# Grouping the weighted sums of a fused attention and expert kernel, with a fourth probability buffer

## The chip, the cores and the metric

The kernel runs on one core of a Trainium2 chip. The metric is the device time of one launch in microseconds (us), median of three runs.

## The reference

For x of 4 batches x 1024 tokens x 256 features, both branches read the layer-normalised rows `xn`; attention has 16 heads of width 16, and each token goes to 2 of 8 experts.

```python
xn = _layernorm(x, axis=-1)
x = x + attn(xn, Wq, Wk, Wv, Wo, bo) + ffn(xn, router_logits, gating_einsum, linear, per_expert_scale, router_scale)
# attn
scores = jnp.einsum('bhqd,bhkd->bhqk', q, k)          # causal, plus the ALiBi bias, / sqrt(D)
w = jax.nn.softmax(scores, axis=-1)
ctx = jnp.einsum('bhqk,bhkd->bqhd', w, v).reshape(b, s, e)
return ctx @ Wo + bo
# ffn: softmax over 8 experts, top 2, then per expert
activation = jax.nn.gelu(gate_out[:, 0, :]) * gate_out[:, 1, :]
expert_outputs = jax.lax.ragged_dot(activation, linear.astype(dtype), group_sizes=tokens_per_expert)
```

## The kernel before, in words

The order of every engine's work is written out by hand; each engine walks its own list and waits on semaphores.

**Projection** (0 to 122.5 us) goes over 8 chunks of 512 tokens. VectorE takes means and variances (`statistics`), GpSimd makes the reciprocal roots from them (`rstds`), VectorE normalises (`normalise`, L464), TensorE transposes, and projects q, k and v. The float32 q and k are split into three bfloat16 parts: ScalarE makes the first two, GpSimd the third (L400), and SyncE stores them in device memory and loads them back as rows of `stacks`.

**Attention** (122.5 to 550 us) has 16 steps `t`, one for each batch and set of four heads. A step is cut into 18 pairs `p`. Each pair issues two score matmul groups (L753, "S" below, 512 columns each, for one head and one of the 9 units of 512 key and query columns) and between them one or two items (L745, "item" below): products for a later step from which VectorE takes row maxima (L707). Item and VectorE share two slots of PSUM: item n is only issued when VectorE is through with item n-2 (`m_taken`). ScalarE takes the exponentials of S into one of three buffers `probs` (L1090), after S has one of three PSUM banks. GpSimd masks the diagonal blocks (L883). The weighted sums (L1152, "V" below) multiply probabilities with values in float32, four heads beside each other in four column tiles of 32; a unit of 512 columns costs 16 matmul records. V of unit u stands behind pair 2u+1, with the low half of unit 2 behind pair 4, its high half and unit 3 behind pair 7: the list `PV_AT` holds nine groups of V a step. VectorE also works through some fifty operations of the routing in steps 0 to 5 (one after each odd pair), and GpSimd scatters the slot map with 8 indirect DMAs a step (L873) in steps 5 to 12. The experts' first weights `w_gu` are loaded by SyncE in steps 5 to 12.

**Experts and combination** (550 us to the end) go over 71 tiles of tokens and then add everything up.

Of the kernel before, what the change touches and what calls it, by code (L numbers as in the profile page):

```python
# [19 lines left out]
P = 128  # L20
# [17 lines left out]
CH = 512  # L38
# [50 lines left out]
PRING = 3  # L89
SRING = 3  # L90

# [11 lines left out]
PV_AT[4], PV_AT[5], PV_AT[7] = [LOW_LAST], [], [HIGH_FIRST, (3, 0), (3, 1)]  # L103
PV_LAST = [[], []] + PV_AT[:-3] + [PV_AT[-3] + PV_AT[-2] + PV_AT[-1]]
# [51 lines left out]
ROWS_AT = {(2, q): (0, (3 * q, 3 * q + 1, 3 * q + 2)) for q in range(2)} | {(4 + k, 1): (1, (2 * k, 2 * k + 1)) for k in range(3)}  # L156
# [93 lines left out]
def project(nc, ctx, ins, scratch, keep, heads, ahead):  # L250
# [64 lines left out]
    def on_sync(sp):  # L315
# [13 lines left out]
        def stores(c, par, load):  # L329
            sp.wait_ge(xn_ready, c + 1)  # L330
            sp.dma_start(xn_rows[ds(c, 1)].rearrange("a p t d -> (a p) t d"), xn[:, par]).then_inc(x_stored[par], 16)
            if load:
                sp.dma_start(x_in[:, c % XR], x_rows[c + XR]).then_inc(x_loaded[c % XR], 16)
            for q in range(NQ):
# [5 lines left out]
                if (c, q) == (2, 0):  # L340
                    for j in range(NQ):
                        sp.wait_ge(parts_stored[j], 16 + 16 * 2)
# [12 lines left out]
    def on_gpsimd(pool):  # L355
# [36 lines left out]
        for c in range(2):  # L392
            rstds(c, c)

        def body(c, par, nxt, i):
            if not nxt:
                ahead["split_maxima"](pool, 0)
            for q in range(NQ):
                pool.wait_ge(p2_ready, 4 * c + q + 1)
                pool.tensor_tensor(parts[:, q, 2], rest[:, q % 2], parts[:, q, 1], ALU.subtract).then_inc(p3_ready, 1)  # L400
            if c + 2 < NC:
                rstds(c + 2, par)

# [4 lines left out]
                           base=S - P, pattern=[[-1, S]], channel_multiplier=1).then_inc(mask_set, 1)  # L408
        early = keep["route"]
# [8 lines left out]
        for k in range(2):  # L418
            for c in range(2):
                pool.iota(keep["entries"][:, k, :, c], pattern=[[P, NT]], base=k * c * TOK, channel_multiplier=1).then_inc(mask_set, 1)  # L420
        chunks(pool, body)
# [174 lines left out]
def attend(nc, ctx, ins, scratch, keep, heads, stored):  # L596
# [3 lines left out]
    qs, ks, vals, probs = heads["qs"], heads["ks"], keep["vals"], keep["probs"]  # L600
# [210 lines left out]
    def on_sync(sp):  # L811
# [7 lines left out]
        def body(t, b, hq, has):  # L819
# [23 lines left out]
            if MAP_FROM <= t < MAP_FROM + NE:  # L843
                e = t - MAP_FROM
# [4 lines left out]
    def on_gpsimd(pool):  # L849
# [26 lines left out]
        def mask_unit(n, u):  # L876
# [4 lines left out]
            for c in DIAG[u]:  # L881
                part = probs[:, u % PRING, :, c:c + P]
# [196 lines left out]
    def on_scalar(act):  # L1079
# [4 lines left out]
        def exp(n, u, h):  # L1084
# [3 lines left out]
            if h == 0:  # L1088
                act.wait_ge(pv_done, n + 1)
# [509 lines left out]
```

## Time and profile before

| | |
|---|---|
| median of 3 runs | 816.59 us (814.65 to 817.5) |
| profiled execution | 818.57 us, span 816.8 us |
| TensorE busy | 768.0 us, 94% |
| VectorE busy | 545.4 us, 67% |
| ScalarE busy | 467.1 us, 57% |
| GpSimd busy | 429.9 us, 53% |
| mean granted TensorE clock | 0.991 |
| chain that ended last | PE 55%, issue 10%, POOL 8%, ACT 4%, DVE 4% |

Start a reading with the chain and the busy shares, and then by stage: from 122.5 to 501.7 us the fourteen attention steps 0 to 13 take 379.2 us, 26.1 to 28.7 us each. A matmul's duration in the profile is longer than its share of the array, since matmuls overlap: the distance from one start to the next is what counts.

### The profile page before, as it was taken

Reading aid. Unit: us, or ns where it says so; the run is one execution under the profiler, and the core shown is the slowest. Engines: PE = TensorE matmul, PEld = TensorE weight load, DVE = VectorE, ACT = ScalarE, POOL = GpSimd, SP = SyncE. Lnnn points to the kernel's source line nnn. Section 1 sums busy time; section 2 is a strip of 40 time slices with the busy share of each in tenths; the row PEclk is TensorE's granted clock in tenths of the full one; section 3 lists DMA queues with packets and bytes.
Section 4 is the critical chain, followed back from the end, with each engine's and each line's share of the span. In section 5 each row is a group of like instructions: output and inputs, shape, how many; then the busy total and the mean of one; then the engine's idle time right before and its main releaser. Section 6 shows DMA issues by size and latency. Waiting matters only on the chain.

```text
span 816.8 us, 17685 instructions
## 1 busy us (share of the span) xinstructions
PE 768.0 (94%) x6172; PEld 470.9 (58%) x6172; DVE 545.4 (67%) x1419; ACT 467.1 (57%) x984; POOL 429.9 (53%) x561
## 2 busy tenths in 40 slices
PE   7899999999999999999999999879899999989997
PEld 5555554444444444444444444329788888888876
DVE  5458879999999887888888888303234434334348
ACT  2565557777778677777777777874233323323310
POOL 5765542231324545645475463255586666666676
PEclk9999999999999999999999999999899999999999
DMA  8786562503233135243342350113533333322777
GB/s 199 229 253 218 170 193 74 157 17 106 82 93 85 52 95 132 51 109 100 110 98 71 94 159 16 37 40 97 139 106 108 112 116 102 111 78 87 234 237 243
DMA packets 74912, 98.20 MB, mean 120 GB/s; under 512 B 16588, under 2 KB 54092, under 8 KB 74764
## 3 DMA queue, kind: packets, MB, share of 16 engines
q1 hardware_dynamic: 65960, 78.34, 34.1%
q0 software_dynamic: 8864, 18.72, 7.4%
q8 instruction: 50, 0.82, 0.4%
q14 instruction: 38, 0.31, 0.1%
HBM read 63.53 MB, written 30.75 MB: 115 GB/s over the span
## 4 chain that ended last, share of the span: by engine, by line
PE 55%; issue 10%; POOL 8%; ACT 4%; DVE 4%; DMA 2%; another core or an unknown queue 1%; DVEq 0%; POOLq 0%; ACTq 0%
PE banks L1152 16%; PE banks L753 15%; PE banks L745 13%; PE banks L1337 7%; POOL expert_rows L1241 4%; ACT probs L1090 4%; PE banks L1346 3%; POOL stacks L592 3%; DVE stacks L1436 2%; DMA stacks<-xn_rows,places 2%; PE banks L1267 1%; DVE junk L707 1%; DMA w_gu<-expert_rows 0%; DVE probs L1319 0%
## 5 line engine op out<-in xcount | busy, mean ns | idle before, releaser
L707 DVE CUSTOM_DVE_ANT_0 junk<-banks,mask 128x128 bf16<-128x128 f32 (+7 forms) x512 | 359.3, 752 | 54.9 <-issue 50.8
L1090 ACT ACTIVATE probs<-banks 128x512 f32<-128x512 f32 x576 | 310.9, 607 | 101.2 <-PE banks L753 93.7
L753 PE MATMUL banks<-stacks 105*128 105x512 bf16 (+3 forms) x768 | 198.8, 328 | 10.5 <-issue 7.8
L745 PE MATMUL banks<-stacks 102*128 102x512 bf16 (+3 forms) x768 | 172.6, 326 | 2.7 <-DVE maxima L707 2.4
L883 POOL TENSOR_SCALAR_AFFINE_SELECT probs<-probs 128x512 f32<-128x512 f32 x128 | 79.6, 640 | 102.3 <-ACT probs L1090 98.3
L1319 DVE TENSOR_TENSOR probs<-banks,probs 128x256 f32<-128x256 f32 x71 | 30.0, 422 | 151.5 <-ACT probs L1283 111.9
L753 PEld LDWEIGHTS banks<-stacks 105*128 105x128 bf16 x768 | 65.5, 97 | 103.5 <-ACT probs L1090 38.0
L1152 PE MATMUL banks<-probs,ctxT 128*17 128x256 f32 (+2 forms) x1920 | 114.4, 360 | 2.0 <-DVE banks L1071 1.1
L1241 POOL DMA_INDIRECT expert_rows<-stacks,places x71 | 77.5, 1091 | 67.9 <-ACT stacks L1288 51.7
L745 PEld LDWEIGHTS banks<-stacks 102*128 102x128 bf16 x768 | 69.0, 98 | 73.1 <-DVE maxima L707 18.5
L1283 ACT ACTIVATE probs<-banks 128x256 f32<-128x256 f32 x71 | 27.3, 384 | 111.9 <-PE banks L1337 56.4
L592 POOL DMA_INDIRECT stacks<-xn_rows,places x71 | 71.7, 1011 | 21.5 <-issue 19.3
L1346 PE MATMUL banks<-stacks,probs 128*128 x284 | 76.2, 392 | 6.7 <-DVE probs L1319 5.8
L1152 PEld LDWEIGHTS banks<-probs,ctxT 128*17 128x17 f32 x1920 | 45.4, 96 | 61.4 <-issue 24.6
L1337 PEld LDWEIGHTS banks<-probs,mask 128*128 128x128 f32 x576 | 70.3, 194 | 4.9 <-issue 2.3
L1337 PE MATMUL banks<-probs,mask 128*128 128x128 f32 x576 | 72.0, 279 | 0.9 <-issue 0.9
L873 POOL DMA_INDIRECT slot_map<-entries,slot x64 | 62.5, 977 | 18.5 <-issue 18.5
L1337 PEld LDWEIGHTS banks<-probs,junk 128*128 128x128 f32 x560 | 68.8, 196 | 4.5 <-issue 2.7
L1337 PE MATMUL banks<-probs,junk 128*128 128x128 f32 x560 | 70.6, 280 | 0.4 <-issue 0.4
L687 POOL TENSOR_SCALAR msplit<-maxima 128x32 bf16<-128x32 f32 x16 | 4.8, 303 | 115.0 <-DVE maxima L707 115.0
L563 PE MATMUL banks<-probs,ctxT 128*128 128x512 f32 x128 | 59.0, 598 | 0.9 <-ACT probs L496 0.9
L1346 PEld LDWEIGHTS banks<-stacks,probs 128*128 128x128 f32 x284 | 49.1, 193 | 13.7 <-issue 9.6
(129 smaller groups left out, 769.6 us busy)
## 6 DMA issues: line engine op xcount, KB each, us to landing
stacks<-qk_parts SPq DMA_DIRECT2D x192, 128.0 KB, 3.1
qk_parts<-ctxT SPq DMA_DIRECT2D x32, 384.0 KB, 3.4
xn_rows<-probs SPq DMA_DIRECT2D x8, 512.0 KB, 5.3
ctxT<-inverse_sums SPq DMA_DIRECT2D x8, 512.0 KB
w_gu<-in_w_gu SPq DMA_DIRECT2D x8, 512.0 KB
stacks<-in_x SPq DMA_DIRECT2D x16, 256.0 KB
ctxT<-expert_rows SPq DMA_DIRECT2D x16, 256.0 KB, 3.1
w_gu<-expert_rows SPq DMA_DIRECT2D x16, 256.0 KB, 5.8
```

What stands on the lines that cost most here:

```text
L563: last = pe.matmul(qkpsum[:, q % 2], w_qk[:, dh, q], xT[:, par, dh], start=dh == 0, stop=dh == DH - 1)
L592: pool.indirect_dma_start(keep["rows"][:, s % RR], None, scratch["xn"], bass.IndirectOffsetOnAxis(ap=keep["places"][:, s, 0:1].bitcast(U32 ...
L707: last = dve.tensor_tensor_reduce(junk[:, n % RING, c:c + w], mpsum[:, slot, c:c + w], keep["mask"][:, S - w:S], 1.0, 3 * NEG, ALU.add, AL ...
L745: last = pe.matmul(mpsum[:, slot, at + c:at + e], qs[hq][0:R_MAX, h, qt * P:(qt + 1) * P], ks[hq][0:R_MAX, h, c:e], start=True, stop=True)
L753: last = pe.matmul(score_bank(("S", n, h))[:, c:c + w], ks[hq][:, h, kt * P:(kt + 1) * P], qs[hq][:, h, q0:q0 + w], start=True, stop=True)
L873: pool.indirect_dma_start(scratch["map"], bass.IndirectOffsetOnAxis(ap=keep["slot"][:, k, i:i + 1].bitcast(U32), axis=0), keep["entries"][ ...
L883: pool.affine_select(out=part, in_=part, compare_op=ALU.is_ge, fill=0.0, base=0, pattern=[[0, 4], [1, P]], channel_multiplier=-1).then_inc ...
L1090: act.activation(probs[:, u % PRING, h], score_bank(("S", n, h)), ACT.Exp, scale=SCALE).then_inc(exp_done, 1)
L1152: last = pe.matmul(cpsum[32 * h:32 * h + VW, q0 % CH:q0 % CH + w], vals[b][:, kt, hq, h], probs[:, u % PRING, h, c:c + w], start=i == 0 an ...
L1241: pool.indirect_dma_start(scratch["y"], bass.IndirectOffsetOnAxis(ap=places[:, s, 1:2].bitcast(U32), axis=0), y[:, s % RR], None).then_inc ...
L1337: last = pe.matmul(gu[:, s % 2, P * c:P * (c + 1)], w_now[s % 2][:, dh, P * c:P * (c + 1)], xT[:, s % 2, dh], start=dh == 0, stop=dh == DH ...
L1346: last = pe.matmul(yp[:, s % 2, 0:D], hT[:, s % 2, dh], w_down[:, ds(e * DH + dh, 1)].rearrange("p a c -> p (a c)"), start=dh == 0, stop=d ...
```

## The change

Four things change. First, steps 0 to 13 issue V in four groups instead of nine: behind pairs 4, 9, 13 and 17 (`PV_GROUPED`). Second, these steps use four probability buffers; the fourth lies in the last quarter of `w_gu`, so the weights of the last two experts are loaded in steps 14 and 15, and those two steps use three buffers again and the old order. Third, GpSimd sets up the mask before the first `rstds` and its other constants between the first and the second, instead of all of them behind the second. Fourth, SyncE loads the first rows of head set 0 one place earlier in chunk 2 of the projection, and in attention it loads the twelve pieces of a head set in three portions, the second and third behind a further finished V unit each.

```diff
-PRING = 3
+PRING = 4
+PROBS = 3
+FEW_FROM = B * NQ - 2
+def prob_buffers():
+    buffer, was, last = [], [], {}
+    for n in range(B * NQ * NU):
+        k = n - NU * FEW_FROM
+        buffer.append(n % PRING if k < 0 else (k + 2) % PROBS)
+        was.append(last.get(buffer[n]))
+        last[buffer[n]] = n
+    return buffer, was
+PROB_BUF, PROB_WAS = prob_buffers()
+PV_GROUPED = [[] for _ in range(PAIRS)]
+PV_GROUPED[4] = [(0, 0), (0, 1), (1, 0), (1, 1), LOW_LAST]
+PV_GROUPED[9] = [HIGH_FIRST, (3, 0), (3, 1), (4, 0), (4, 1)]
+PV_GROUPED[13] = [(5, 0), (5, 1), (6, 0), (6, 1)]
+PV_GROUPED[17] = [(7, 0), (7, 1), (8, 0), (8, 1)]
-ROWS_AT = {(2, q): (0, (3 * q, 3 * q + 1, 3 * q + 2)) for q in range(2)} | {(4 + k, 1): (1, (2 * k, 2 * k + 1)) for k in range(3)}
+ROWS_AT = {(2, 0): (0, (3, 4, 5))} | {(4 + k, 1): (1, (2 * k, 2 * k + 1)) for k in range(3)}
...
+            if c == 2:
+                for j in range(NQ):
+                    sp.wait_ge(parts_stored[j], 16 + 16 * 2)
+                load_rows(sp, scratch, heads, 0, 0, range(3))
...
-        for c in range(2):
-            rstds(c, c)
         mask = keep["mask"]
         pool.memset(mask[:, :], 0.0).then_inc(mask_set, 1)
...
+        rstds(0, 0)
...
+        rstds(1, 1)
...
-    qs, ks, vals, probs = heads["qs"], heads["ks"], keep["vals"], keep["probs"]
+    qs, ks, vals = heads["qs"], heads["ks"], keep["vals"]
+    probs = [keep["probs"][:, i] for i in range(PROBS)] + [Room(keep["w_gu"][:, 3 * NE * DH // 4:].rearrange("p e h -> p (e h)"))([P, 4, CH])]
...
-                sp.wait_ge(pv_done, PRING + NU * t)
-                load_quad(sp, scratch, heads, *quad(b, hq, 3))
+                for k in range(3):
+                    sp.wait_ge(pv_done, PRING + NU * t + k)
+                    load_rows(sp, scratch, heads, *quad(b, hq, 3), (2 * k, 2 * k + 1))
...
-            if MAP_FROM <= t < MAP_FROM + NE:
-                e = t - MAP_FROM
+            if t >= FEW_FROM:
+                sp.wait_ge(pv_done, PRING + NU * FEW_FROM)
+            for e in [t - MAP_FROM] if MAP_FROM <= t < MAP_FROM + 3 * NE // 4 else [NE - B * NQ + t] if t >= FEW_FROM else []:
...
-            if h == 0:
-                act.wait_ge(pv_done, n + 1)
-            act.activation(probs[:, u % PRING, h], score_bank(("S", n, h)), ACT.Exp, scale=SCALE).then_inc(exp_done, 1)
+            if h == 0 and PROB_WAS[n] is not None:
+                act.wait_ge(pv_done, PRING + PROB_WAS[n] + 1)
+            act.activation(probs[PROB_BUF[n]][:, h], score_bank(("S", n, h)), ACT.Exp, scale=SCALE).then_inc(exp_done, 1)
...
-                for u0, half in PV_AT[p] if has(1) else PV_LAST[p]:
+                for u0, half in (PV_GROUPED if t < FEW_FROM else PV_AT if has(1) else PV_LAST)[p]:
```

What this moves on TensorE, in pairs 5 to 9 of a step: before, V stands behind pair 7 (12 rows: one and a half units) and again behind pair 9.

```order
758 L753 MATMUL banks<-stacks 128x512
759 L745 MATMUL banks<-stacks 128x512 x2
760 L753 MATMUL banks<-stacks 128x512 x2
761 L745 MATMUL banks<-stacks 128x512
762 L745 MATMUL banks<-stacks 128x384
763 L745 MATMUL banks<-stacks 128x128
764 L753 MATMUL banks<-stacks 128x512 x2
765 L745 MATMUL banks<-stacks 128x512
766 L745 MATMUL banks<-stacks 128x256 x2
767 L753 MATMUL banks<-stacks 128x512
768 L1152 MATMUL banks<-probs,ctxT 17x256 x12
769 L753 MATMUL banks<-stacks 128x512
```

And now, from the same pair 5 on (S is L778, items L770, V L1179):

```order
741 L778 MATMUL banks<-stacks 128x512
742 L770 MATMUL banks<-stacks 128x512 x2
743 L778 MATMUL banks<-stacks 128x512 x2
...
751 L770 MATMUL banks<-stacks 128x512
752 L770 MATMUL banks<-stacks 128x128
753 L770 MATMUL banks<-stacks 128x384
754 L778 MATMUL banks<-stacks 128x512 x2
755 L770 MATMUL banks<-stacks 128x512 x2
756 L778 MATMUL banks<-stacks 128x512
757 L1179 MATMUL banks<-probs,ctxT 17x256 x12
758 L1179 MATMUL banks<-w_gu,ctxT 17x256 x8
```

The group behind pair 7 has moved behind pair 9 and joined the one there: five pairs with five items stand in a row, and then two and a half units of V.

On GpSimd at the start of the program, before: the constants stand behind both `rstds` and ahead of the first third parts (L400).

```order
22 L372 TENSOR_SCALAR ctxT<-ctxT 128x4
...
28 L387 TENSOR_SCALAR ctxT<-ctxT 128x4
29 L405 MEMSET mask 128x1024
30 L407 AFFINE_SELECT mask<-mask 128x1024
31 L410 IOTA w_gu 128x8
...
37 L420 IOTA entries 128x32 x4
38 L400 TENSOR_TENSOR ctxT<-ctxT 128x512 x4
```

And now (mask L417 and L419, the other constants L423 to L433, third parts L441):

```order
15 L417 MEMSET mask 128x1024
16 L419 AFFINE_SELECT mask<-mask 128x1024
17 L396 TENSOR_SCALAR ctxT<-ctxT 128x4
...
23 L411 TENSOR_SCALAR ctxT<-ctxT 128x4
24 L423 IOTA w_gu 128x8
...
30 L433 IOTA entries 128x32 x4
31 L396 TENSOR_SCALAR ctxT<-ctxT 128x4
...
37 L411 TENSOR_SCALAR ctxT<-ctxT 128x4
38 L441 TENSOR_TENSOR ctxT<-ctxT 128x512 x4
```

The first third part now stands directly behind the second `rstds`.

## Rows read from the trace of the kernel before

**Rows 1.** Windows: stretch, length, busy us (count) by engine, clock, DMA, GB/s.

```profile
122.50:282.70 160.20, 157.73 (x1544) 70.06 (x1544) 154.50 (x454) 123.49 (x236) 49.08 (x87) 1.00 0.31 85
282.70:501.70 219.00, 211.10 (x2061) 93.21 (x2057) 181.52 (x517) 162.57 (x313) 117.74 (x172) 1.00 0.37 95
203.10:229.20 26.10, 25.95 (x261) 11.81 (x257) 25.52 (x80) 20.48 (x39) 9.15 (x16) 1.00 0.25 69
311.40:338.80 27.40, 26.33 (x261) 11.70 (x257) 22.43 (x65) 20.27 (x39) 16.56 (x23) 1.00 0.34 93
```

**Rows 2.** Timeline, step 7, pairs 9 to 11: start, length, engine, instruction.

```profile
326.28 1.06 PE L1152 MATMUL banks<-probs,ctxT 128*17 128x256 f32 x16
327.27 0.39 PE L753 MATMUL banks<-stacks 105*128 105x512 bf16 x1
...
328.81 0.38 PE L753 MATMUL banks<-stacks 105*128 105x512 bf16 x1
329.12 0.63 PE L1152 MATMUL banks<-probs,ctxT 128*17 128x256 f32 x8
```

**Rows 3.** Timeline, step 8, pairs 5 to 8, and a VectorE row of pair 12.

```profile
347.04 0.39 PE L753 MATMUL banks<-stacks 105*128 105x512 bf16 x1
...
349.19 0.08 DVE L707 DVE_READ_ACCUMULATOR2_ANT maxima<- 128x1 f32 x1
349.19 1.08 DVE L707 CUSTOM_DVE_ANT_0 junk<-banks,mask 128x896 bf16<-128x896 f32 x1
349.33 0.61 PE L745 MATMUL banks<-stacks 102*128 102x512 bf16 x3
349.78 0.38 PE L753 MATMUL banks<-stacks 105*128 105x512 bf16 x1
350.09 1.49 PE L1152 MATMUL banks<-probs,ctxT 128*17 128x256 f32 x24
...
350.42 0.95 DVE L707 CUSTOM_DVE_ANT_0 junk<-banks,mask 128x768 bf16<-128x768 f32 x1
...
351.51 0.39 PE L753 MATMUL banks<-stacks 105*128 105x512 bf16 x1
351.74 0.60 PE L745 MATMUL banks<-stacks 102*128 102x512 bf16 x3
...
352.51 0.82 DVE L707 CUSTOM_DVE_ANT_0 junk<-banks,mask 128x640 bf16<-128x640 f32 x1 [0.79 <-issue]
...
358.33 0.96 DVE L707 CUSTOM_DVE_ANT_0 junk<-banks,mask 128x768 bf16<-128x768 f32 x1 [0.42 <-issue]
```

**Rows 4.** Timeline, first pair of step 3 (ACT) and of step 8 (PE, ACT).

```profile
203.57 0.60 ACT L1090 ACTIVATE probs<-banks 128x512 f32<-128x512 f32 x1 [0.61 <-PE banks L753]
...
338.83 0.39 PE L753 MATMUL banks<-stacks 105*128 105x384 bf16 x2
...
340.40 0.60 ACT L1090 ACTIVATE probs<-banks 128x512 f32<-128x512 f32 x1 [1.60 <-PE banks L753]
```

**Rows 5.** Timeline of the first chunk: GpSimd, then VectorE, then TensorE.

```profile
5.69 0.25 POOL L372 TENSOR_SCALAR ctxT<-ctxT 128x4 f32<-128x4 f32 x1 [2.74 <-DVE ctxT L456]
...
12.96 0.23 POOL L372 TENSOR_SCALAR ctxT<-ctxT 128x4 f32<-128x4 f32 x1 [3.48 <-DVE ctxT L456]
...
16.69 0.95 POOL L405 MEMSET mask<- 128x1024 f32 x1
...
21.51 2.26 POOL L400 TENSOR_TENSOR ctxT<-ctxT 128x512 bf16<-128x512 f32 x2
...
16.61 3.95 DVE L464 TENSOR_SCALAR probs<-w_gu,ctxT 128x256 f32<-128x256 f32 x4
...
28.69 1.38 DVE L464 TENSOR_SCALAR probs<-w_gu,ctxT 128x256 f32<-128x256 f32 x4 [2.29 <-issue]
...
20.62 1.09 PE L540 MATMUL banks<-ident,probs 128*128 128x128 f32 x8 [1.83 <-DVE probs L464]
...
25.58 2.11 PE L573 MATMUL banks<-ctxT,probs 128*128 128x264 f32 x8 [2.09 <-ACT logits L526]
```

More of the change, by code:

```diff
@@ L339, in stores @@
                     ahead["maxima_rows"](sp, 0, 0)
-                if (c, q) == (2, 0):
-                    for j in range(NQ):
-                        sp.wait_ge(parts_stored[j], 16 + 16 * 2)
                 if (c, q) in ROWS_AT:
@@ L391, in on_gpsimd @@
         pool.iota(unused[:, :, 2], pattern=[[0, NST]], base=0, channel_multiplier=0).then_inc(unused_set, 1)
-        for c in range(2):
-            rstds(c, c)
[L395 to L402, printed above, removed]
         mask = keep["mask"]
@@ L420, in on_gpsimd, with body @@
                 pool.iota(keep["entries"][:, k, :, c], pattern=[[P, NT]], base=k * c * TOK, channel_multiplier=1).then_inc(mask_set, 1)
+        rstds(1, 1)
+        def body(c, par, nxt, i):
+            if not nxt:
+                ahead["split_maxima"](pool, 0)
+            for q in range(NQ):
+                pool.wait_ge(p2_ready, 4 * c + q + 1)
+                pool.tensor_tensor(parts[:, q, 2], rest[:, q % 2], parts[:, q, 1], ALU.subtract).then_inc(p3_ready, 1)
+            if c + 2 < NC:
+                rstds(c + 2, par)
         chunks(pool, body)
@@ L881, in mask_unit @@
             for c in DIAG[u]:
-                part = probs[:, u % PRING, :, c:c + P]
+                part = probs[PROB_BUF[n]][:, :, c:c + P]
                 pool.affine_select(out=part, in_=part, compare_op=ALU.is_ge, fill=0.0, base=0,
@@ L1151, in weighted @@
                 for h in range(4):
-                    last = pe.matmul(cpsum[32 * h:32 * h + VW, q0 % CH:q0 % CH + w], vals[b][:, kt, hq, h], probs[:, u % PRING, h, c:c + w],
+                    last = pe.matmul(cpsum[32 * h:32 * h + VW, q0 % CH:q0 % CH + w], vals[b][:, kt, hq, h], probs[PROB_BUF[n]][:, h, c:c + w],
                                      start=i == 0 and (u, half) in ((0, 0), HIGH_FIRST),
@@ L1481, in build @@
         heads = head_buffers(nc, ctx, keep["stacks"])
-        keep["probs"] = sb("probs", [P, PRING, 4, CH])
+        keep["probs"] = sb("probs", [P, PROBS, 4, CH])
         last_vals = sb("last_vals", [P, KT, NQ, 4, VW])
```

## The prediction

> **What bounds the kernel now.** I read the windows by stage first. In steps 6 to 13 TensorE is busy 211 of 219 us, in steps 0 to 5 it is busy 158 of 160 [rows 1]. The reader is to see the next column in the same rows as well: VectorE is busy 154 of 160 us in steps 0 to 5, and in step 3, which takes 26.1 us, it is free for 0.6 us. In step 7, without routing, it still has 22.4 us of work in 27.4 [rows 1]. So there are two engines near their limit, joined by two PSUM slots, and the question is what lumping TensorE's work does to the second one. The timeline of single pairs answers that, which I read next.
>
> **TensorE's own work in a step.** The S in front of V starts 0.31 us before it [rows 2]; three item matmuls that stream 1024 columns take 0.45 us from start to start [rows 3], so 512 columns take 0.22 and the entry into a V group costs 0.09. V of one unit (x16) takes 0.99 us to the next S [rows 2], V of one and a half units (x24) takes 1.42 [rows 3]: half a unit is 0.43, a unit 0.86, and the exit costs 0.13 to 0.14. A group thus costs 0.23 us beside its columns. Two pairs lie between 327.27 and 329.12 [rows 2], less the entry 0.88 us a pair. Sum of a step: 18 x 0.88 + 9 x 0.86 + 9 x 0.23 = 25.6 us, and step 3 takes 26.1. With four groups it would be 24.5.
>
> The Trainium skill (TensorEngine Tiling (Array Packing), Key Properties) says that a change of tiling mode drains TensorE; this trace agrees, with 0.09 and 0.14 us at the two ends of a V group. By that rule alone the change takes 5 x 14 = 70 switches away; what they are worth is my first rival below.
>
> **What grouping does between TensorE and VectorE.** Item n waits for VectorE's item n-2. Rows 3 hold each piece. VectorE's items follow each other 1.23 us apart (349.19 to 350.42). TensorE issues the next item 0.06 us after VectorE's last read of the one before (349.19 + 0.08 to 349.33). VectorE starts 0.77 us behind the item's first matmul (351.74 to 352.51). From the last item to V it is 0.76 us (349.33 to 350.09). Count from the first S of a run of pairs, with VectorE empty: its first item is issued at 0.23, VectorE takes it from 1.00 to 2.23, so the third item is issued at 2.29 where TensorE alone would have it at 1.99; the fourth is at 3.52, the fifth at 4.75. A run of three pairs exists now: 2.29 + 0.76 + 1.28 + 0.14 = 4.47, and it takes 4.47 us (347.04 to 351.51) [rows 3].
>
> VectorE then has nothing until the next run's first item. Its last two items last about 1.23 us each from the release on, so its idle time is V minus 0.5 us: 0.35 for one unit and 0.78 for one and a half, where the trace has 0.42 and 0.79 [rows 3].
>
> After the change the runs have 5, 5, 4 and 4 pairs, followed by V of 2.13, 2.13, 1.71 and 1.71 us. Five pairs: 4.75 + 0.76 + 2.13 + 0.14 = 7.78. Four pairs: 3.52 + 0.76 + 1.71 + 0.14 = 6.13. A step: 2 x 7.78 + 2 x 6.13 = 27.8 us. VectorE idles 1.6, 1.6, 1.2 and 1.2 us in it, which with 22.4 us of work gives 28.0, the same within rounding. TensorE loses 3.3 us a step to waits on VectorE and wins 1.15 by fewer switches. Fourteen steps: 389.5 us.
>
> The fourth buffer does its part: with it the exponentials never wait for a V behind them (unit 6 needs V of unit 2, which opens the group before it), so I count no wait there. It moves nothing either, since ScalarE is not what is late.
>
> **Routing.** In steps 0 to 5 VectorE has some fifty more operations, one behind each odd pair; the two stretches of rows 1 give 154.5 / 6 - 22.4 = 3.3 us a step. Most will now fall into the idle 5.6 us of a step. Only those behind pairs 1 and 5 stand before an item that the last item of a run waits for. 3.3 / 9 is 0.37 each; some are longer, and I take 0.45: 2 x 0.45 x 6 = 5.4 us. Ends: 0 (all hidden) and 3.3 x 6 = 20 us (none).
>
> **Late releases beside GpSimd's scatters.** In step 3, whose first S is where the window starts (203.1), ScalarE follows it by some 0.45 us (203.57). In step 8 it follows by 1.57 us (338.83 to 340.40), and step 7 takes 27.4 us where step 3 takes 26.1 [rows 1, 4]. This stands in steps 6 to 13 only, behind V of unit 8, where the slot map is scattered. I have no mechanism for it. Rows 4 bound one such delay at 1.1 us. Ends: none at all after the change, or one at each of four groups in eight steps, 35 us. I take half a microsecond a step, 4 us, as V is no longer at the same place against the scatters.
>
> **Sum of attention.** Steps 0 to 13 take 160.2 + 219.0 = 379.2 us [rows 1]. After: 389.5 + 5.4 + 4 = 398.9. That is 19.7 us more. Steps 14 and 15 keep their order.
>
> **The start of the projection.** GpSimd waits 2.74 us and 3.48 us for the first two variances [rows 5]. The mask's two operations, 16.69 to 18.8, fit into the first wait, the others, 18.8 to 21.5, into the second. GpSimd is ready again before either wait ends, so there they cost nothing, unless they stretch VectorE's statistics beside them (nothing in the trace shows that meeting; at most the 2.57 us that L464 suffers). What goes: VectorE's four L464 take 3.95 us beside these constants, 1.38 in the next chunk [rows 5]; L400 starts at 21.51 and could start at 16.7. TensorE idles 1.83 us for the one and 2.09 us for the chain L400, L483, L505, L526 behind the other [rows 5]. If both go, 3.9 us. I take the gain to stay, as TensorE is the busiest engine of the chunks behind. What is late next: L400 will now run beside L464, a meeting that this trace does not show. Ends: 0 and -4 us; I take -3.3: one of the four L464 stretched, where three suffered 2.57 us in sum, and a part of that hidden.
>
> The Trainium skill (SBUF — State Buffer, Who interferes with whom) says that VectorE's `tensor_scalar` can hold a port pair that GpSimd needs too, and that the second to issue blocks fully. The trace agrees for the constants, 3.95 against 1.38 us, but L464 beside GpSimd's tiny L383 keeps its 1.38 us. By the rule L400 would stretch L464 again, some 2.3 us would be left of the 3.9, and my sum would end at 834.
>
> **Edits at nothing.** SyncE's portions: the second and third wait for V of units 0 and 1, now behind pair 4; behind them in the queue stands only the row of maxima, which is due in pair 16, and the rows themselves are for the next step's pair 10. The rows of chunk 2 leave one place earlier in a queue that no engine waits for. The last two `w_gu` blocks land in steps 14 and 15, while VectorE is done with its items, and the experts begin at 550 us, some 20 us behind the start of step 15. If that cover failed, the time of one 512 KB load would show.
>
> **The sum.** 19.7 - 3.3 = 16.4 us on the profiled execution of 818.57 us (span 816.8): 835.0. That execution lies 2.0 us above the median of 816.6, so the median goes to 833.0 us. Slower, by 2%.
>
> **Rivals.**
> 1. *TensorE alone is the bound, the switches are the gain* (faster). Each of the 14 steps goes down by 1.15 us, and the start by 3.3: 816.6 - 16.1 - 3.3 = 797. For it speaks 94 to 98% of TensorE in rows 1; against it VectorE's 0.6 us of free time in step 3, and the run of three pairs, which already waits 0.3 us. It decides from the item time: my waits of 3.3 us a step hang on ten item times in a row (3, 3, 2, 2), they would fall to the 1.15 us saved plus the 0.5 us lost today if an item took 1.07 us instead of 1.23. Chance 0.08.
> 2. *The late releases go with the regrouping, and VectorE catches up while V runs* so that each step costs 27.1 as steps 8 to 13 do now. 14 x 27.1 = 379.4, nothing against today, and the start gives 3.3: 813.5. For it: the 1.1 us of rows 4 is as large as the gain of my sum in a step. Against: two slots hold only 2.46 us of work. Chance 0.09.
> 3. *The late releases multiply*: a V group is longer and meets a scatter more often, at two groups a step of 1.1 us: 8 x 2.2 - 4 = 13.6 more, 847. Chance 0.09.
> 4. My forecast: 0.74.
>
> **How the numbers follow.** The forecast's own range: routing 0 to 12 in place of 5.4, late releases 0 to 9 in place of 4, start 0 to -4: 823 to 843. It leaves out rival 1, rival 3 and part of rival 2, a little over 2 in 10, so I open it to 821 and 845. This kernel's measurement can tell 0.3%, 2.5 us, from no change. Faster by more: rival 1 and half of rival 2, 0.12. Within: 0.06. Slower: 0.82.
>
> **What would show it.** Right: steps of about 27.8 us in steps 7 to 13, four idle times of VectorE a step of 1.6, 1.6, 1.2 and 1.2 us, items in pairs 2 to 4 and 7 to 9 released 0.06 us behind VectorE's read, S of step 0 near 119 us, L464 of chunk 1 at 1.4 us. Wrong: VectorE's idle time below 0.8 us behind a long group, steps below 27 us, or the exponentials waiting for V.

## The result and the profile after

The changed kernel takes 835.87 us (median of 6 runs, 834.54 to 837.46), the kernel before, run beside it, 817.05 us (6 runs). The ratio is 1.0228, interval 1.0203 to 1.0253. The forecast of 833.0 us lies 0.3% below it, inside its range. Its profiled execution has a span of 834.4 us, 17.6 above the one before.

Windows of the changed kernel: start of the program, steps 0 to 5, steps 6 to 13, step 3, step 9, and from the end of attention on. Columns as in [rows 1].

```profile
0.00:123.95 123.95, 116.19 (x444) 67.60 (x444) 79.34 (x221) 62.94 (x149) 71.18 (x120) 0.97 0.70 208
123.95:299.00 175.05, 160.63 (x1544) 71.27 (x1545) 155.21 (x457) 121.73 (x236) 50.31 (x88) 1.00 0.28 78
299.00:524.87 225.87, 214.46 (x2061) 95.47 (x2057) 178.66 (x516) 159.64 (x312) 118.04 (x172) 1.00 0.34 88
211.30:240.24 28.94, 26.70 (x261) 11.85 (x258) 25.41 (x78) 20.16 (x39) 9.19 (x15) 1.00 0.20 58
383.70:411.94 28.24, 26.84 (x261) 11.93 (x258) 22.13 (x64) 20.00 (x39) 16.60 (x24) 1.00 0.33 89
571.54:834.42 262.88, 240.21 (x1687) 220.46 (x1686) 115.23 (x189) 80.03 (x213) 171.36 (x154) 0.99 0.45 138
```

Against [rows 1], step 3 goes from 26.1 to 28.94 us with the same instructions in it, and VectorE's work in it does not change (25.52 to 25.41). By stage, before and after:

| us | before | after | change | forecast |
|---|---|---|---|---|
| start of step 0 | 122.5 | 123.9 | +1.4 | -3.3 |
| steps 0 to 13 | 379.1 | 400.9 | +21.8 | +19.7 |
| steps 14, 15 | 48.4 | 46.7 | -1.7 | 0 |
| experts to the end | 266.8 | 262.9 | -3.9 | 0 |

So the sum came out close in part because misses of opposite sign met: in this pair of profiles the start got later instead of earlier and the stages behind step 13 got shorter. The expert stage is no work saved. Inside it TensorE's granted clock was at half (1.2 in place of 2.4 GHz) for 10.2 us before and 3.4 us after; at half speed that is up to 3.4 us of the 3.9.

Half of the 1.7 us in steps 14 and 15 is an effect of the change that the forecast did not have: step 14 goes from 25.31 to 24.44 us. Before, VectorE copies the first tile's expert weights (L1303) while GpSimd splits the last row maxima, and TensorE waits for these. VectorE's copy waits until all of `w_gu` has landed, so with the later loads it waits 17.8 us and GpSimd is alone. The same operation of GpSimd takes 0.69 us beside the copy and 0.25 us without it. Timelines of step 14, before and then after:

```profile
518.56 0.69 DVE L1303 COPY mask<-w_gu 128x1024 f32 x1 [1.16 <-issue]
518.67 0.69 POOL L693 TENSOR_TENSOR mrest<-mrest,msplit 128x32 f32<-128x32 f32 x1
...
520.31 0.23 PE L731 MATMUL banks<-ident_b,msplit 128*96 128x128 bf16 x1 [1.25 <-POOL msplit L695]
```

```profile
541.85 0.25 POOL L718 TENSOR_TENSOR mrest<-mrest,msplit 128x32 f32<-128x32 f32 x1
...
542.62 0.23 PE L756 MATMUL banks<-ident_b,msplit 128*96 128x128 bf16 x1 [0.38 <-POOL msplit L720]
```

On one chip step 14 takes 25.32 us without the later loads (e3 and e4 below) and 24.44 with them (e1 and e2).

Timeline of the changed kernel, step 9, pairs 5 to 9 (S L778, items L770, VectorE's reading L732, V L1179). It answers [rows 3].

```profile
391.80 0.39 PE L778 MATMUL banks<-stacks 105*128 105x512 bf16 x1
392.03 0.60 PE L770 MATMUL banks<-stacks 102*128 102x512 bf16 x2
...
392.80 1.23 DVE L732 CUSTOM_DVE_ANT_0 junk<-banks,mask 128x1024 bf16<-128x1024 f32 x1 [1.66 <-issue]
392.90 0.60 PE L770 MATMUL banks<-stacks 102*128 102x512 bf16 x3
393.20 4.79 ACT L1117 ACTIVATE probs<-banks 128x512 f32<-128x512 f32 x9
...
393.86 0.10 PEld L778 LDWEIGHTS banks<-stacks 105*128 105x128 bf16 x1 [0.48 <-ACT probs L1117]
...
394.09 0.61 PE L770 MATMUL banks<-stacks 102*128 102x512 bf16 x3
...
395.31 0.61 PE L770 MATMUL banks<-stacks 102*128 102x512 bf16 x3
...
396.54 0.61 PE L770 MATMUL banks<-stacks 102*128 102x512 bf16 x2 [0.18 <-DVE maxima L732]
...
397.29 0.62 PE L1179 MATMUL banks<-w_gu,ctxT 128*17 128x256 f32 x8
...
399.57 0.39 PE L778 MATMUL banks<-stacks 105*128 105x512 bf16 x1
```

The run of five pairs goes as counted out: from the first S at 391.80 the third, fourth and fifth item stand at 2.29, 3.51 and 4.74 us (forecast 2.29, 3.52, 4.75), V at 5.49, the next S at 7.77 (7.78). VectorE idled 1.66 us ahead of the run. The other long idle times of step 9 are 1.46, 1.77 and 1.23 us; 1.6, 1.6, 1.2 and 1.2 were forecast, their sum 6.1 against 5.6. One thing stands here that the forecast did not have: S waits too, 0.48 us, for ScalarE, which runs nine exponentials back to back at 0.53 us each. Whether that costs time is the business of three experiments below (e6, e7 and e12).

Timeline of the first pair of step 9, answering [rows 4]:

```profile
383.70 0.39 PE L778 MATMUL banks<-stacks 105*128 105x384 bf16 x2
...
384.75 0.60 ACT L1117 ACTIVATE probs<-banks 128x512 f32<-128x512 f32 x1 [2.21 <-PE banks L778]
```

ScalarE starts 1.05 us behind S, where it is 0.43 in steps 1 to 5 and 1.57 in [rows 4]. The late release is still there, once a step in steps 6 to 13, and it makes the first run of step 9 take 5.81 us (V at 389.51) where the second takes 5.49.

Timeline of the start, answering [rows 5] (statistics' roots L396, normalise L488, third parts L441, first parts L525, rest L507, projection L587; SPq is SyncE's queue):

```profile
11.12 0.40 SPq L354 DMA_DIRECT2D xn_rows<-probs  x1
...
15.64 2.21 DVE L488 TENSOR_SCALAR probs<-w_gu,ctxT 128x256 f32<-128x256 f32 x4
...
16.54 2.33 POOL L441 TENSOR_TENSOR ctxT<-ctxT 128x512 bf16<-128x512 f32 x2
...
22.56 3.60 PE L587 MATMUL banks<-probs,ctxT 128*128 128x512 f32 x8
...
26.11 1.38 DVE L488 TENSOR_SCALAR probs<-w_gu,ctxT 128x256 f32<-128x256 f32 x4 [4.61 <-DMA xn_rows<-probs]
28.41 0.60 ACT L525 ACTIVATE ctxT<-banks 128x512 bf16<-128x512 f32 x1 [5.11 <-DMA qk_parts<-ctxT]
...
29.79 6.78 PE L587 MATMUL banks<-probs,ctxT 128*128 128x512 f32 x8 [3.63 <-DVE ctxT L507]
...
41.13 7.03 PE L587 MATMUL banks<-probs,ctxT 128*128 128x512 f32 x16
```

The intended gain is there: chunk 1 is projected from 22.56 us on, where it was 27.52, and L488 beside the third parts takes 2.21 us, not 3.95. Then it is lost. Chunk 0's rows, handed to the queue at 11.12, land at 26.0, 14.9 us later; VectorE waits 4.61 us for them, ScalarE 5.11 for chunk 0's parts, TensorE 3.63. Behind that idle time its clock is at half from 29.2 to 36.0 us: eight matmuls take 6.78 us where eight took 3.60. Chunk 2 starts at 41.13, against 39.11 before. One profile of each kernel is a thin basis for a difference of 1.4 us in the start, though; the experiments below add more of both.

### The profile page after: what moved, and what is told of

It is laid out like the page before. It is cut to its first block and busy times, and to the rows that moved or that the text cites. A ratio compares the mean times of both kernels' runs of the same rounds, so it can differ in the third digit from the quotient of the medians.

```text
span 834.4 us, 17681 instructions
## 1 busy us (share of the span) xinstructions
PE 772.9 (93%) x6172; PEld 472.1 (57%) x6172; DVE 542.8 (65%) x1419; ACT 462.2 (55%) x984; POOL 429.9 (52%) x561
## 3 DMA queue, kind: packets, MB, share of 16 engines
q1 hardware_dynamic: 65960, 78.34, 33.3%
## 5 line engine op out<-in xcount | busy, mean ns | idle before, releaser
L732 DVE CUSTOM_DVE_ANT_0 junk<-banks,mask 128x128 bf16<-128x128 f32 (+7 forms) x512 | 357.1, 753 | 79.6 <-issue 58.8
L1117 ACT ACTIVATE probs<-banks 128x512 f32<-128x512 f32 x452 | 243.0, 614 | 96.1 <-PE banks L778 90.0
L778 PE MATMUL banks<-stacks 105*128 105x512 bf16 (+3 forms) x768 | 193.4, 328 | 10.4 <-ACT probs L1117 3.7
L770 PE MATMUL banks<-stacks 102*128 102x512 bf16 (+3 forms) x768 | 173.5, 327 | 18.3 <-DVE maxima L732 15.1
L770 PEld LDWEIGHTS banks<-stacks 102*128 102x128 bf16 x768 | 61.8, 97 | 105.0 <-DVE maxima L732 57.7
L778 PEld LDWEIGHTS banks<-stacks 105*128 105x128 bf16 x768 | 65.4, 97 | 97.5 <-issue 33.8
L910 POOL TENSOR_SCALAR_AFFINE_SELECT probs<-probs 128x512 f32<-128x512 f32 x101 | 63.3, 645 | 91.0 <-ACT probs L1117 87.2
L1117 ACT ACTIVATE w_gu<-banks 128x512 f32<-128x512 f32 x124 | 69.1, 611 | 30.7 <-PE banks L778 29.0
L1179 PE MATMUL banks<-probs,ctxT 128*17 128x256 f32 (+2 forms) x1440 | 80.3, 359 | 0.0
L587 PE MATMUL banks<-probs,ctxT 128*128 128x512 f32 x128 | 62.3, 625 | 4.6 <-DVE ctxT L507 3.6
L441 POOL TENSOR_TENSOR ctxT<-ctxT 128x512 bf16<-128x512 f32 x32 | 37.1, 1160 | 43.1 <-ACT ctxT L529 43.1
```

The costliest lines, as they stand in the source:

```text
L587: last = pe.matmul(qkpsum[:, q % 2], w_qk[:, dh, q], xT[:, par, dh], start=dh == 0, stop=dh == DH - 1)
L732: last = dve.tensor_tensor_reduce(junk[:, n % RING, c:c + w], mpsum[:, slot, c:c + w], keep["mask"][:, S - w:S], 1.0, 3 * NEG, ALU.add, AL ...
L770: last = pe.matmul(mpsum[:, slot, at + c:at + e], qs[hq][0:R_MAX, h, qt * P:(qt + 1) * P], ks[hq][0:R_MAX, h, c:e], start=True, stop=True)
L778: last = pe.matmul(score_bank(("S", n, h))[:, c:c + w], ks[hq][:, h, kt * P:(kt + 1) * P], qs[hq][:, h, q0:q0 + w], start=True, stop=True)
L910: pool.affine_select(out=part, in_=part, compare_op=ALU.is_ge, fill=0.0, base=0, pattern=[[0, 4], [1, P]], channel_multiplier=-1).then_inc ...
L1117: act.activation(probs[PROB_BUF[n]][:, h], score_bank(("S", n, h)), ACT.Exp, scale=SCALE).then_inc(exp_done, 1)
```

## The experiments

The experiments ran on three chips, e1 to e4, e5 to e8 and e9 to e12 together. The kernel before takes 789.1, 816.1 and 824.6 us on them; ratios are to its runs on the same chip. Step 3, which has routing but no late release, can be compared across chips: in every kernel with whole items and exponentials it takes 26.1 us with nine groups and 28.94 us with four.

### Which part of the change does it

`e1_nine_groups`, the changed kernel with the old groups:

```diff
-                for u0, half in (PV_GROUPED if t < FEW_FROM else PV_AT if has(1) else PV_LAST)[p]:
+                for u0, half in (PV_AT if has(1) else PV_LAST)[p]:
```

> The changed kernel with V in nine groups in every step again; the fourth buffer, SyncE's portions and both edits of the start stay. Theory (the long runs of pairs empty VectorE's two slots, that is the loss): steps 0 to 13 return from 401 us to about 379 us, the median to 816 to 818 us. Rival (the fourth buffer or the portions cost something themselves): it stays above 822 us.

`e2_grouping_alone`: the kernel before with `prob_buffers`, `PV_GROUPED`, the portions in attention and the later `w_gu` loads (their part of the diff as shown ahead); GpSimd's and SyncE's start as before.

> The changed kernel with the start as before: GpSimd's constants behind both rstds, the row loads in their old place. Theory: the grouping keeps all of its 22 us in steps 0 to 13, and step 0 begins at 122.5 us again instead of 123.9, so 834 to 836 us. If the start edits have a real gain that the profiled execution only missed by chance, this is slower than the changed kernel by up to 3 us.

`e3_constants_alone`: the kernel before with only GpSimd's constants placed anew.

```diff
-        for c in range(2):
-            rstds(c, c)
...
+        rstds(0, 0)
...
+        rstds(1, 1)
```

> The kernel before with GpSimd's constants alone placed anew. Theory: chunk 1 starts some 4 us earlier on TensorE, then waits for the store of chunk 0's rows and parts, which the DMA queues only land at 26 to 28 us; TensorE sits idle for over 3 us and its granted clock falls to half for 6 to 7 us. Step 0 begins at 123 to 124 us, the median is 816 to 819 us. As predicted at first (a gain of 3.3 us): 813.5 us.

`e4_constants_and_queue`: the same, with x of chunk 3 and the eight loads of bias rows moved out of the first 11 us.

```diff
-        for i in range(1, XR):
+        for i in range(1, XR - 1):
...
+            if c == 0:
+                sp.dma_start(x_in[:, XR - 1], x_rows[XR - 1]).then_inc(x_loaded[XR - 1], 16)
...
+            if c == 1:
+                for q in range(NQ):
+                    sp.dma_start(heads["qs"][q][R_ALIBI:R_MAX, :, :], ins["c_q"][q]).then_inc(heads["const_in"], 16)
```

> The kernel before with GpSimd's constants placed anew, and SyncE's queue of the start relieved: x of chunk 3 is loaded behind the store of chunk 0's rows, and the ALiBi constants (480 KB in eight loads) behind the stores of chunk 1. Theory (the new wait is on a backlog of the DMA queues): the wait for the row store and the clock drop go, step 0 begins at 117.5 to 119.5 us, the median is 812 to 814 us. If the backlog is not the cause, it is where e3 is.

Measured, on one chip (before: 789.12 us, 26 runs):

| | us | ratio (interval) | start of step 0 | steps 0 to 13 |
|---|---|---|---|---|
| e1 nine groups, the rest of the change | 784.87 | 0.995 (0.993 to 0.9971) | 119.6 | 370.6 |
| e2 grouping alone | 815.89 | 1.0329 (1.0305 to 1.0353) | 124.3 | 398.4 |
| e3 constants alone | 786.63 | 0.9969 (0.9951 to 0.9988) | 122.4 | 370.5 |
| e4 constants and loads | 790.06 | 1.0006 (0.9987 to 1.0025) | 127.0 | 370.6 |

Windows of e1 and of e2, both steps 6 to 13 and the step 9 inside them:

```profile
279.53:490.23 210.70, 209.23 (x2061) 92.92 (x2057) 181.49 (x517) 163.84 (x312) 118.06 (x172) 1.00 0.38 94
...
358.77:385.03 26.26, 26.12 (x262) 11.66 (x258) 22.48 (x65) 20.48 (x39) 16.61 (x24) 1.00 0.46 106
```

```profile
299.32:522.71 223.39, 213.65 (x2061) 94.89 (x2057) 177.98 (x516) 160.64 (x312) 117.98 (x172) 1.00 0.35 89
...
383.09:411.01 27.92, 26.70 (x261) 11.84 (x258) 22.05 (x64) 20.08 (x39) 16.61 (x24) 1.00 0.37 92
```

The grouping alone costs 27.8 us of attention (398.4 less 370.6), more than the whole change in the two profiles above, and everything else of the change together gains half a per cent. The changed kernel itself was not run on this chip. The fourth buffer, the portions and the late weights (all in e1) cost nothing in steps 0 to 13: 370.6 us with them, 370.5 without. No run groups with three buffers, so whether the fourth is needed was not tested.

On this chip nothing of the late releases is to be seen: ScalarE follows the first S of every step from 1 on by 0.43 us, steps 6 to 13 take 26.3 us each with nine groups, and with four 27.9, where the forecast without late releases was 27.8. The scatters are the same in every kernel, so they alone do not make a release late; what differs between the chips was not settled. Set against this chip, the late releases cost 8.3 us in the kernel before (219.0 less 210.7 us for steps 6 to 13) and only 2.5 in the changed one (225.9 less 223.4). On the third chip it is 14.8 with nine groups (e11) and 8.1 with four (e10). That is why the whole change costs 21.8 us of attention in the profiles above and the grouping alone 27.8 here: a grouped kernel loses less to late releases. That its own waits cover part of them would explain it, but is not shown.

The start was not what was expected in any of these. With the constants alone VectorE waits 3.36 us for chunk 0's rows, TensorE idles 2.4 us at 29 and has its clock at half for 3.4 us, as expected; yet the median is 2.5 us below the kernel before (0.9 to 3.9 us by the interval), where no gain was expected and the forecast's own 3.3 us lies inside. With nine groups and the same constants the clock stays up, and step 0 begins at 119.6. And e2, which starts like the kernel before, has step 0 at 124.3, as TensorE waits 5.09 us for ScalarE (L549) and its clock is at half from 25.7 to 29.2 us. So the start varies from profile to profile, whichever order the constants have. All profiles of kernels with the loads in their old place, those of the next section too (e5 to e8 differ from chunk 3 on by their short items):

| constants | chunk 2 projected from, us | step 0 starts, us | clock at half before 40 us, us |
|---|---|---|---|
| old place (before, e2, e5, e8) | 39.1, 40.8, 41.1, 38.7 | 122.5, 124.3, 124.3, 121.6 | 0, 3.4, 6.8, 0 |
| new place (after, e1, e3, e6, e7, e9, e12) | 41.1, 36.8, 39.0, 40.5, 40.9, 39.3, 39.9 | 123.9, 119.6, 122.4, 121.5, 121.8, 122.5, 122.8 | 6.8, 0, 3.4, 6.8, 6.8, 3.4, 3.4 |

With the constants in the new place VectorE waits 3.4 to 4.6 us for chunk 0's rows in six profiles of seven, and in none of the four with the old one. Step 0 starts at 122.1 us on average against 123.2. The wait is shown; that it makes the start later than before is not.

e4 takes the first wait away (chunk 2 is projected from 35.43 us) and pays for it two chunks later. Timeline of e4, around chunk 3 (L467 normalise, L504 first parts, L566 projection):

```profile
49.48 1.38 DVE L467 TENSOR_SCALAR probs<-w_gu,ctxT 128x256 f32<-128x256 f32 x4 [3.72 <-DMA xn_rows<-probs]
52.70 0.60 ACT L504 ACTIVATE ctxT<-banks 128x512 bf16<-128x512 f32 x1 [4.95 <-DMA qk_parts<-ctxT]
...
54.08 3.78 PE L566 MATMUL banks<-probs,ctxT 128*128 128x512 f32 x4 [3.47 <-DVE ctxT L486]
```

The order of the queue suggests a second backlog: eight loads behind chunk 1 and twelve loads of rows around chunk 2's parts. TensorE idles 3.47 us, and its clock is at half from 53.4 to 63.6 us.

### Is it VectorE's turn, and what comes behind it

The forecast hangs on an item costing VectorE 1.23 us, and rival 1 names 1.07 us as the point from which grouping should pay. Four kernels cut the work of an item or of an exponential, in both orders of V. Only parts of the maxima and of the probabilities are then computed.

`e5_before_short_items` and `e6_after_short_items` (the same edit in both kernels):

```diff
-            last = dve.tensor_tensor_reduce(junk[:, n % RING, c:c + w], mpsum[:, slot, c:c + w], keep["mask"][:, S - w:S], 1.0, 3 * NEG,
+            m = w - max(P, w // 2)
+            last = dve.tensor_tensor_reduce(junk[:, n % RING, c + m:c + w], mpsum[:, slot, c + m:c + w], keep["mask"][:, S - w + m:S], 1.0, 3 * NEG,
```

> The kernel before, with VectorE reading only the last half (at least 128) of the columns of every item, so that an item costs it 0.6 to 0.8 us in place of 1.23; the maxima are then those of part of the columns. My theory (VectorE's turn through two PSUM slots sets the grouped kernel): nothing but TensorE bounds nine groups now, steps of 25.6 us in steps 0 to 13, 358 us for the fourteen, no waits of items. A rival, that TensorE alone bounded it already: steps 6 to 13 stay where they are in the kernel before on the same chip.

> The changed kernel with the same short items. Prediction as it stands on record (break-even at an item of 1.07 us, TensorE the only other bound): steps 24.5 us, fourteen steps 15 us shorter than with nine groups and short items. Rival A, that a grouped step is long for another reason than items (switches, the fourth buffer in w_gu): steps stay at 27.9 and the fourteen 20 us longer. Rival B, ScalarE and its three banks of S take over: step 9 of the changed kernel has S waiting for L1117, ScalarE needs 0.53 us for an S where TensorE issues one each 0.44, so of the ten S of a five-pair run the last ones wait; counted through, 25.3 us a step, and the gain over nine groups with short items is 4 us, not 15.

`e7_after_short_items_and_exps` and `e8_before_short_items_and_exps` have this as well (e8 with the old buffer's name), and `e12_after_short_exps` has this alone:

```diff
-            act.activation(probs[PROB_BUF[n]][:, h], score_bank(("S", n, h)), ACT.Exp, scale=SCALE).then_inc(exp_done, 1)
+            act.activation(probs[PROB_BUF[n]][:, h, 0:CH if n < NU else CH // 2], score_bank(("S", n, h))[:, 0:CH if n < NU else CH // 2], ACT.Exp, scale=SCALE).then_inc(exp_done, 1)
```

> The changed kernel with short items and, from step 1 on, exponentials of only half the columns (some 0.32 us in place of 0.53; the rest of the probabilities are old ones). If ScalarE is the second wait: steps 1 to 13 at 24.5 us, 11 us below the run with short items alone, and 15 below nine groups with the same two. If it is not: the same as with short items alone.

> The kernel before with short items and short exponentials. ScalarE has 2.1 us of S in 2.85 us of two pairs there, so it is not late: every theory gives the same steps as with short items alone, 25.6 us. If steps shrink too, ScalarE is late even with nine groups.

> The changed kernel with whole items and, from step 1 on, exponentials of half the columns. Theory: VectorE is what runs of five pairs wait for, ScalarE's waits lie in its shadow and come to the fore only with short items; steps 7 to 13 stay within 0.2 us of the changed kernel's. Rival: ScalarE's banks (0.48 us of wait for L1117 at one S) add to it; then a step loses up to 1 us, 14 us in all.

Measured (e12 on the third chip, beside e10 with its whole exponentials: 28.94 in step 3):

| | us | ratio (interval) | step 3, nine groups | step 3, four groups |
|---|---|---|---|---|
| whole items, whole exponentials | | | 26.1 (before) | 28.94 (after) |
| short items | 812.81; 808.54 | 0.9951 (0.9925 to 0.9977); 0.9908 (0.9874 to 0.9943) | 26.05 (e5) | 26.13 (e6) |
| short exponentials | 846.39 | 1.0272 (1.024 to 1.0305) | | 28.87 (e12) |
| both short | 799.96; 786.42 | 0.9807 (0.978 to 0.9835); 0.9612 (0.957 to 0.9653) | 25.58 (e8) | 24.54 (e7) |

Windows of step 3: of e6, then of e7, then of e12.

```profile
200.40:226.53 26.13, 25.68 (x262) 12.04 (x258) 17.79 (x78) 19.51 (x39) 8.97 (x15) 1.00 0.23 65
```

```profile
197.46:222.00 24.54, 24.54 (x261) 12.45 (x257) 17.30 (x78) 13.21 (x39) 9.22 (x15) 1.00 0.24 70
```

```profile
210.10:238.97 28.87, 26.14 (x261) 11.92 (x257) 25.34 (x78) 13.22 (x39) 9.00 (x15) 1.00 0.20 58
```

Short items take 2.8 us from a grouped step and nothing from an ungrouped one: what grouping cost is VectorE's turn, shown. (That an ungrouped step stays at 26.05 us, where 25.6 was expected of e5, has the same reason as what follows: with short exponentials too, in e8, it takes 25.58, so with nine groups ScalarE costs half a microsecond as well.) Short exponentials alone take next to nothing from the grouped kernel (28.87 for 28.94, and steps 7 to 13 within 0.2 us of e10's on average), so the 0.48 us of S for L1117 in the timeline above is not a cost of the changed kernel: it ends before the item's own wait does. But with short items the grouped kernel is no better than the ungrouped one (steps 0 to 13 take 375.7 and 375.0 us), though an item now lasts some 0.8 us, well under the 1.07 that I gave. Timeline of e6, step 3, pairs 5 to 7 (S L779, items L771, exponentials L1118):

```profile
209.56 2.08 ACT L1118 ACTIVATE w_gu<-banks 128x512 f32<-128x512 f32 x4
...
209.74 0.10 PEld L779 LDWEIGHTS banks<-stacks 105*128 105x128 bf16 x1 [0.48 <-ACT probs L1118]
...
210.72 0.10 PEld L779 LDWEIGHTS banks<-stacks 105*128 105x128 bf16 x1 [0.32 <-ACT w_gu L1118]
...
211.69 0.10 PEld L779 LDWEIGHTS banks<-stacks 105*128 105x128 bf16 x1 [0.38 <-ACT w_gu L1118]
```

Every pair of the run now waits for ScalarE, which takes S at 0.53 us through three banks, where TensorE issues two in 0.88. The four runs of step 3 take 4.99, 4.99, 4.17 and 3.69 us; with short exponentials 4.48, 4.55, 3.64 and 3.59. Only e7, with both consumers short, reaches the 24.5 us that the forecast gives as TensorE's own, 1.04 below nine groups. Over steps 0 to 13 e7 takes 356.7 us and e8 367.4, 10.7 apart where 15 was expected. Rival B of e6 was right in kind; its 25.3 us was 0.8 too low, and its 4 us of gain were none.

### How it goes with the number of groups

`e9_six_groups`, the changed kernel with

```diff
-PV_GROUPED[9] = [HIGH_FIRST, (3, 0), (3, 1), (4, 0), (4, 1)]
-PV_GROUPED[13] = [(5, 0), (5, 1), (6, 0), (6, 1)]
+PV_GROUPED[7] = [HIGH_FIRST, (3, 0), (3, 1)]
+PV_GROUPED[9] = [(4, 0), (4, 1)]
+PV_GROUPED[11] = [(5, 0), (5, 1)]
+PV_GROUPED[13] = [(6, 0), (6, 1)]
```

> The changed kernel with six groups of V a step in place of four: behind pairs 4 (2.5 units), 7 (1.5), 9, 11, 13 (1 each) and 17 (2). My model (TensorE's own times, an item every 1.23 us through two slots, an S every 0.53 us through three banks) counts 25.9 us for nine groups, 26.9 for six and 27.8 for four. So on this chip the fourteen steps lie 14 us below the changed kernel's and some 14 above nine groups' before routing and late releases; three switches fewer than nine groups buy 0.7 us a step and lose 1.7. If the switches were what counts, six groups would lie at the same time as nine or below.

Measured: 847.88 us, ratio 1.0269 (1.0235 to 1.0304), beside 824.56 for the kernel before. The order of the three lies as counted in steps 0 to 5, where no release is late: 160.3 us with nine groups (e11), 168.4 with six, 175.0 with four (e10). Step 3 takes 27.7 us, between 26.1 and 28.9, and step 11, without routing, 27.1 (26.9 forecast). The sum over fourteen steps does not hold: 406.1 us, as much as four groups on this chip (406.5, e10). Windows of step 6 and of step 7:

```profile
290.90:324.40 33.50, 29.53 (x262) 12.45 (x259) 22.89 (x65) 20.33 (x39) 15.73 (x24) 0.90 0.38 90
324.40:352.50 28.10, 26.30 (x261) 11.74 (x257) 22.31 (x64) 20.05 (x39) 15.09 (x22) 1.00 0.29 79
```

Step 6 has a granted clock of 0.90. Its first late release leaves TensorE idle for 1.11 us (at 293.67, for L1119), a second one for 1.24 us (at 317.58), and the clock is at half from 296.1 to 299.5 and from 320.0 to 323.4 us; steps 10 and 12 go the same way (31.6 and 33.3 us). No other run here has its clock fall inside steps 0 to 13. Why this order invites it, when e11 below has idle times of the same size in the same steps and keeps the clock, stays open.

### Can the start be mended

`e10_after_loads_later`, the changed kernel, and `e11_nine_groups_loads_later`, e1, each with

```diff
-            if load:
-                sp.dma_start(x_in[:, c % XR], x_rows[c + XR]).then_inc(x_loaded[c % XR], 16)
...
+            if load:
+                sp.dma_start(x_in[:, (c + XR - 1) % XR], x_rows[c + XR - 1]).then_inc(x_loaded[(c + XR - 1) % XR], 16)
+            for k in {0: (0, 1), 2: (2, 3)}.get(c, ()):
+                sp.dma_start(heads["qs"][k][R_ALIBI:R_MAX, :, :], ins["c_q"][k]).then_inc(heads["const_in"], 16)
+                sp.dma_start(heads["ks"][k][R_ALIBI:ROWS, :, :], ins["c_k"]).then_inc(heads["const_in"], 16)
```

the added lines behind chunk c's parts, and the bias rows' loads ahead of the first chunk gone.

> The changed kernel with 1.5 MB of loads moved out of the first 25 us: x of chunk c+3 is loaded behind chunk c's parts, the bias rows of head sets 0 and 1 behind chunk 0's parts, those of 2 and 3 behind chunk 2's. Theory (the start term failed because the transfers of chunk 0 land late, 4.61 us of wait for the xn rows and 5.11 for the parts): both waits fall below 2.5 us, TensorE keeps its full clock between 29 and 36 us, S of step 0 starts at 118 to 119 us, 4 to 5 below the changed kernel. Rival: the backlog only moves to chunks 1 to 3, as when the bias rows went there alone, and the start is at 122 or later.

> Nine groups with everything else of the change, and the loads placed as in the run before. Expected: steps as in the kernel before, start at 118 to 119, so the kernel before less some 4 us and a ratio of 0.992 to 0.996, the best version of the study. Rival: start at 122, ratio 0.998 to 1.001.

Measured: 851.19 us, ratio 1.0337 (1.0304 to 1.037), and 826.77 us, ratio 1.0026 (1.0007 to 1.0044). Step 0 starts at 125.5 and 124.6, where 118 to 119 was expected. Timeline of e10:

```profile
23.56 7.03 PE L587 MATMUL banks<-probs,ctxT 128*128 128x512 f32 x16
35.15 7.03 PE L587 MATMUL banks<-probs,ctxT 128*128 128x512 f32 x16
46.73 5.31 PE L587 MATMUL banks<-probs,ctxT 128*128 128x512 f32 x12
...
60.73 1.03 PE L770 MATMUL banks<-stacks 102*128 102x512 bf16 x2 [5.57 <-DMA stacks<-in_c_k]
...
68.34 1.88 PE L587 MATMUL banks<-probs,ctxT 128*128 128x512 f32 x4
```

For three chunks it is what I wanted: no wait for a landing, the clock up, chunk 2 at 35.15 and chunk 3 at 46.73, where the kernel before has 39.11 and 50.69 and the changed one 41.13 and 52.72. So some 4 us can be had at chunk 3 once the loads are out of the way. Then the first item, which waits for the bias rows of all four head sets, meets loads that went out at 50.3 to 52.5 us into a busy queue: 5.57 us of idle TensorE, half clock from 57.2 to 64.0, and chunk 4 at 68.34 against 65.31. That was my placement, not the change, and the rival of both expectations, that the backlog only moves, was right. A wait on head set 0's rows alone, or the second pair of loads one chunk earlier, was not tried.

The best version that computes everything is e1: nine groups and everything else of the change. It takes 0.5% less than the kernel before (0.3 to 0.7% by the interval), and 3.8% less than e2, the grouping alone, on the same chip. Of its 4.2 us against the kernel before, 0.9 is step 14; the rest is the start and what one profile cannot tell from chance.

## Why the prediction was right

- *VectorE's turn through two slots*: right. Run by run 7.78 and 6.13 us were forecast. The second run of step 9 takes 7.77, the third 6.24, the last 6.13 (4.27 and V of 1.86); the first takes 8.10 with its late release and 7.78 in e2, which has none. Items go out 0.06 us behind VectorE's read, as forecast. Steps without routing and late releases take 27.9 us (e2) for 27.8. e6 shows the cause, by taking the cost away with the item.
- *Routing*: mis-sized. The first six steps take 175.05 us, 8.2 above six of 27.8, where 5.4 was forecast. The places are mainly the two that were named: against the 5.49 us of an undisturbed run of five pairs, the first run of these steps takes 0.3 to 1.0 us more and the second 0.3 to 0.6, where 0.45 was taken for each.
- *Late releases*: right in size by luck. Steps 6 to 13 take 225.87 us, 3.5 above eight of 27.8; 4 was taken, as a guess without a mechanism. On one chip late releases are absent; on another the same steps take 231.49 us (e10), 9 above. The forecast also did not see that the 379.2 us it starts from hold 8.3 us of them: the first half of rival 2, that they go with the regrouping, was right for most of them.
- *The start*: the term that failed. "I take the gain to stay" left out what would be late next: the transfers of chunk 0, whose landings nobody had waited for while chunk 1 was late itself. It looked at the engines and not at the queue, though the queue had 2 MB of x, the weights and eight small loads ahead of the rows. In the profile TensorE's idle time went as forecast (chunk 1 5.0 us earlier) and 3.63 us of it came back one chunk later, with a fall of the clock behind them. So step 0 starts 1.4 us later and not near 119 us. The size is open: over the profiles above the start is 1.1 us earlier on average, and e3's median is lower by 2.5 us.
- *L400's new neighbour*: right. One of the four L488 is stretched, to 1.25 us beside 0.40 for the others, and the four take 2.21 us, 0.83 above their usual 1.38. The Trainium skill (SBUF — State Buffer, Who interferes with whom) has it that the second to issue blocks fully; the trace agrees for this one, which starts at 16.60 us, while GpSimd's third part runs from 16.54 to 17.70, and ends at 17.85. How many meet such an operation varies: two in e1, none in e3.
- *Rival 1's point of 1.07 us*: wrong. It counted the next bound as TensorE, and it is ScalarE with three banks. The forecast does not hang on it, only the advice it implies.
- *Fourth buffer, portions, late weights and rows at nothing*: right for steps 0 to 13 (e1). Not quite elsewhere: the late weights take 0.9 us from step 14, and from chunk 3 to chunk 4 of the projection TensorE takes 14.05 us after and in e1, where the kernels without the row edit take 14.6 to 14.7 (before, e3, e2).
- *Sum*: +16.4 forecast, +17.6 measured. Steps 2.1 us too low and the start 4.7 too low, less 5.6 us of later stages, of which 0.9 is the change and the rest clock and chance. The cause and the size of the main term were right; that the whole lies within a third of a per cent is luck.

## What to carry to other kernels

Work that TensorE does by itself is not only a cost: laid between products that others read, it is the time in which these others catch up. Before lumping it together, count each consumer's turn over the longest run without it (here 1.23 us per item through two slots, and behind it 0.53 per S through three), since the second one takes over as soon as the first is mended. And when an early stage gets faster, ask which transfers it will now wait for: list what is ahead of them in the queue. Last, do not judge a stage from one profile of each kernel: here chunk 2 is projected from anywhere between 38.7 and 41.1 us in four kernels whose code is the same up to there.

## What the runs showed of the hardware

- Idle time of TensorE is often followed by half clock, but not always. Behind 3.63 us of waiting at 26 to 30 us it was at half for 6.8 us, behind 5.57 us for 6.8 us (e10), behind 5.09 us for 3.4 us (e2), and in e9 behind 1.11 us for 3.4 us. Waits of 1.1 to 1.25 us in steps 6, 8, 10 and 12 of e11 left it alone.
- The kernel before takes 789, 816 and 825 us on three chips. Steps 0 to 5 are alike (159.9 to 160.3 us with nine groups). The experts' stage (246 to 248, 263 to 267 and 269 to 270 us) and the late releases in steps 6 to 13 make the difference: ScalarE follows the first S of these steps by 0.43 us on the first chip and by 0.8 to 2.2 us on the third.
- VectorE and GpSimd slow each other. GpSimd's subtraction of 128x32 takes 0.24 us alone and 0.69 us beside VectorE's copy of 128x1024 (e1 and e3, step 14); VectorE's `tensor_scalar` of 128x256 takes 0.40 us alone and 1.25 us beside GpSimd's subtraction of 128x512.
- The Trainium skill (TensorEngine Tiling (Array Packing), Key Properties) has the drain at a change of tiling mode. e7 against e8, where TensorE is busy throughout step 3 in both, gives its price here: 25.58 - 24.54 = 1.04 us for five groups, ten changes, fewer, so 0.1 us a change.
